# Fill and drain of a 41-beat pipeline: QKV products ahead of attention, spikes on GpSimd, filler products, four expert banks at the end

## The reference

```python
R, K, V = x @ Wr.T, x @ Wk.T, x @ Wv.T
r, k, v = lif(R), lif(K), lif(V)      # v = v + (x - v)/2 ; s = v >= 1 ; v = v*(1 - s), in time
h = 0.9*h + k*v ; y = r*h             # in time
x1 = LN1(x + y @ Wo.T)
s1 = lif(x1 @ W1.T + b1)              # width 1024
s2 = lif(s1 @ W2.T + b2)
x3 = LN(x + LN2(x1 + s2))             # LN3 in the kernel
g  = softmax(x3 @ Wg + bg) ; keep the top 2 of 8, renormalise
out = LN(x3 + sum_e g_e * (x3 @ We_e + be_e))    # all 8 experts are computed
```

## Time and profile before

| | us |
|---|---|
| median of 3 runs (lowest, highest) | 984.44 (983.77, 984.57) |
| the profiled execution's own time | 983.85 |
| its span, first to last instruction | 982.0 |
| granted TensorE clock, mean | 0.982 |

### The profile page before, as it was taken

How to read it: one execution, slowest core, us unless ns; L and a number is a source line. 1 busy time by engine, 2 the same in 40 slices (tenths; PEclk the granted TensorE clock), 3 DMA queues, 4 the chain that set the end, 5 groups by cost and what they waited for, 6 DMA issues and landing times.

```text
span 982.0 us, 20629 instructions
## 1 busy us (share of the span) xinstructions
PE 930.3 (95%) x6520; PEld 860.4 (88%) x6520; DVE 916.3 (93%) x3683; ACT 610.6 (62%) x1388; POOL 572.8 (58%) x730
## 2 busy tenths in 40 slices
PE   6878899999999999999999999999999999999985
PEld 5778789999999999999999999999999999788764
DVE  7699999999999999999999999999999999989865
ACT  6556455676666666766666667666666676555451
POOL 2222225666667766666677666667776666664552
PEclk9789999999999999999999999999999999999998
DMA  9543223455555544565555545655555455446763
GB/s 285 127 97 66 55 54 65 97 119 119 119 125 108 112 106 99 121 118 119 123 107 105 114 100 121 120 118 122 105 112 107 100 124 108 100 95 112 142 123 86
DMA packets 59293, 109.45 MB, mean 111 GB/s; under 512 B 6576, under 2 KB 6576, under 8 KB 59184
## 3 DMA queue, kind: packets, MB, share of 16 engines
q0 software_dynamic: 37584, 68.44, 40.8%
q1 hardware_dynamic: 16992, 31.30, 9.6%
q10 hardware_dynamic: 4608, 8.39, 2.3%
HBM read 31.29 MB, written 8.39 MB: 40 GB/s over the span
## 4 chain that ended last, share of the span: by engine, by line
PE 76%; DVE 14%; ACT 3%; issue 3%; DMA 2%; POOL 2%; SPq 0%; POOLq 0%; ACTq 0%; DVEq 0%
PE ps_e L405 29%; PE ps_proj L405 12%; PE ps_proj L480 10%; PE ps_proj L495 10%; PE ps_proj L501 5%; PE ps_attn L405 3%; DVE U L898 3%; DVE V L905 2%; PE ps_zx L459 2%; DVE stats L977 2%; PE ps_attn L459 1%; PE ps_attn L442 1%; DVE h L947 1%; DMA acc<-term 1%; POOL rstd L1337 1%
## 5 line engine op out<-in xcount | busy, mean ns | idle before, releaser
L405 PE MATMUL ps_e<-we_hi,x_hi 128*128 128x512 f32 (+2 forms) x640 | 229.6, 359 | 6.4 <-DVE acc L1120 2.8
L898 DVE SCALAR_TENSOR_TENSOR U<-V,U 128x256 f32<-128x256 f32 (+4 forms) x576 | 229.0, 398 | 3.9 <-ACT U L669 2.3
L905 DVE SCALAR_TENSOR_TENSOR V<-U 128x256 f32<-128x256 f32 (+4 forms) x576 | 225.5, 392 | 1.6
L405 PE MATMUL ps_e<-we_lo,x_hi 128*128 128x512 f32 (+2 forms) x640 | 224.0, 350 | 0.0
L405 PE MATMUL ps_e<-we_hi,x_lo 128*128 128x512 f32 (+2 forms) x640 | 223.2, 349 | 0.0
L1335 POOL TENSOR_SCALAR veps<-mv 128x2 f32<-128x2 f32 x128 | 49.7, 388 | 275.5 <-DVE mv L983 273.6
L1349 POOL TENSOR_SCALAR s<-U 128x256 fp32r<-128x256 f32 x208 | 192.8, 983 | 16.5 <-DVE V L905 16.5
L708 ACT ACTIVATE term<-ps_e,gate 128x256 f32<-128x256 f32 x372 | 160.3, 475 | 52.0 <-PE ps_e L405 50.9
L669 ACT ACTIVATE U<-ps_proj,cst 128x256 f32<-128x256 f32 x320 | 135.5, 480 | 70.5 <-PE ps_proj L501 62.0
L405 PEld LDWEIGHTS ps_e<-we_hi,x_hi 128*128 128x128 f32 x640 | 120.6, 188 | 22.6 <-DVE x_lo L1027 3.7
L654 ACT ACTIVATE U<-ps_proj 128x512 f32<-128x512 f32 x96 | 57.6, 600 | 129.7 <-PE ps_proj L405 129.7
(11 more groups left out here) (111 smaller groups left out, 2313.5 us busy)
## 6 DMA issues: line engine op xcount, KB each, us to landing
acc<-term POOLq DMA_DIRECT2D x93, 256.0 KB, 3.7
odd_sum<-term POOLq DMA_DIRECT2D x93, 256.0 KB, 3.3
xt<-x_T SPq DMA_DIRECT2D x33, 256.0 KB, 3.0
xa<-x_tok SPq DMA_DIRECT2D x32, 256.0 KB, 3.3
xb<-cst SPq DMA_DIRECT2D x32, 256.0 KB, 2.3
xb<-x_tok POOLq DMA_DIRECT2D x32, 256.0 KB, 6.1
xt<-x_hi POOLq DMA_DIRECT2D x31, 256.0 KB, 4.6
out<-res ACTq DMA_DIRECT2D x31, 256.0 KB, 2.0
```

Of the source, the lines that this page charges most:

```text
L405: mm = pe.matmul(dst, lhs, rhs, start=(i == 0), stop=(i == n - 1))
L898: v.scalar_tensor_tensor(out=U[:, s, t, c0:c1], in0=V[:, c0:c1], scalar=0.5, in1=U[:, s, t, c0:c1], op0=ALU.mult, op1=ALU.add).then_inc(do ...
L905: v.scalar_tensor_tensor(out=V[:, c0:c1], in0=u, scalar=THRESHOLD, in1=u, op0=ALU.is_lt, op1=ALU.mult).then_inc(done, 1)
```

## The change

It leaves beats 7 to 32 as they are and alters both ends.

* Beat 1: TensorE runs 46 filler matmuls into an unused bank ahead of attention, 4 ahead of x1_T, 8 after it and 8 more in `w1` ahead of the wait for `x1_lo`. VectorE has a table of its own, `FIRST_Y`, with the LN1 sum in slot 6, and `x1_low` in slot 23. ScalarE normalises and reads x1 earlier; the copy of Wo moves to the end of its beat, ahead of `low_x`.
* Beats 2 to 6: `rkv` part 0 (beat 2) or parts 0 and 1 (beats 3 to 6) come first in TensorE's beat, ahead of z_T and attention. From beat 3 on, `x1_T` comes after `w2`, and on ScalarE `read_x1` comes after `to_lif` of w2. `low_x` moves up, ahead of the third w1 part. GpSimd makes six of the eight spike tiles, at the head of its beat; VectorE makes two, in slot 2. LN1's sum, statistics and shift are in slots 4 to 10, `x1_low` in 19 (beat 6: 15).
* Drain: VectorE's `fin_stage` 0 to 3 move up in beats 33 and 34, and GpSimd adds term 7 ahead of LN3's deviation. Beats 35 to 37 (`tail`) have new lists on all engines: expert fills use four banks (two of `ps_e`, two of `ps_proj`), `expert0` comes after the experts and after z_T, terms 4 and 5 are added a beat earlier, and the scan of beat 35 runs in one piece between `fin_stage` 3 and the low half of x3. In beat 37 ScalarE and a DMA take fills 0 and 1, VectorE adds the others.

```diff
+BRIDGE_ATTN, BRIDGE_T, BRIDGE_W1 = 46, 4, 8
...
-FILL = dict(z_sum=-1, y=(-1,) * 5, spikes_h1=-1, fin_sum=-1,
+FILL = dict(z_sum=-1, y=(-1,) * 5, spikes_h1=2, fin_sum=-1,
             gate=(4, 5, 6, 7, 8, 10, 10, 11, 11, 12, 24, 26), add_e0=(13, 14),
-            ln1_sum=1, ln1_stats=(2, 3), ln1_aggr=4, ln1_norm=7, x1_low=17,
+            ln1_sum=4, ln1_stats=(5, 6), ln1_aggr=7, ln1_norm=10, x1_low=19,
             ln2_stats=(0, 0), ln2_aggr=1, ln2_scale=(5, 6), ln2_add=9,
...
             fin_add=24, fin_stats=25, fin_aggr=26, fin_shift=31)
-X1_LOW = {3: 19, 4: 19, 6: 15}
-DRAIN = dict(z_sum=-1, y=(-1,) * 5, spikes_h1=-1, fin_sum=11,
+FIRST_Y = dict(FILL, ln1_sum=6, ln1_stats=(7, 8), ln1_aggr=9, ln1_norm=13)
+X1_LOW = {1: 23, 6: 15}
+DRAIN = dict(z_sum=-1, y=(-1,) * 5, spikes_h1=-1, fin_sum=9,
              gate=(-1, -1, -1, -1, 0, 1, 2, 3, 4, 4, 6, 7), add_e0=(11, 12),
              ln1_sum=-1, ln1_stats=(-1, -1), ln1_aggr=-1, ln1_norm=4, x1_low=-1,
...
              ln3_stats=9, ln3_aggr=10, ln3_shift=14, x3_low=23,
-             fin_add=25, fin_stats=26, fin_aggr=27, fin_shift=31)
-TAIL = dict(DRAIN, add_e0=(5, 5), ln2_scale=(3, 4), x3_low=17)
+             fin_add=17, fin_stats=18, fin_aggr=19, fin_shift=31)
...
     def dve_spikes(self):
-        return FK if self.edge else 0
+        return FK if self.late else 2 if self.early else 0
...
+        def expert_bank(b, fill):
+
+            if not b.tail:
+                return ps_e[:, (b.slot(LAG_M, 2) * (E - 1) + fill) % 2]
+            i = ((E - 1) * (b.k - FIRST_TAIL) + fill) % 4
+            first = (FIRST_TAIL - LAG_M) * (E - 1) % 2
+            return ps_e[:, (first + i) % 2] if i < 2 else ps_proj[:, i - 2]
...
+                        if b.k == LAG_Y and f == 0 and e == 0:
+                            bridge(ps_e[:, 0, 0, :], BRIDGE_W1)
                         for k in range(DK):
                             if f == 0 and e == 0:
                                 pe.wait_ge(x1_lo_ready, b.value(DK, LAG_Y, k + 1))
...
             def expert(b, fill):
-                if some(b.value(E - 1, LAG_M, fill - 1)):
+                if b.tail and (b.k > FIRST_TAIL or fill > 1):
+                    if b.k == FIRST_TAIL and fill < 4:
+                        pe.wait_ge(proj_read, b.fills())
+                    elif b.last_m and fill == E - 2:
+                        pe.wait_ge(last_added, fill - 4 - 1)
+                    else:
+                        pe.wait_ge(term_ready, b.value(E - 1, LAG_M, fill - 3))
+                elif some(b.value(E - 1, LAG_M, fill - 1)):
                     pe.wait_ge(term_ready, b.value(E - 1, LAG_M, fill - 1))
-                bank = (b.slot(LAG_M, 2) * (E - 1) + fill) % 2
+                bank = expert_bank(b, fill)
...
+            def tail(b):
+
+                for part in (0, 1, 2, 3):
+                    expert(b, part)
+                if b.last_m:
+                    gates_T(b)
+                    for part in (4, 5):
+                        expert(b, part)
+                    biases(b)
+                    expert(b, 6)
+                    return
+                expert(b, 4)
+                gates_T(b)
+                x3_T(b)
+                for part in (5, 6):
+                    expert(b, part)
+                biases(b)
+                after = Beat(b.k + 1)
+                if after.has(LAG_Z):
+                    z_T(after)
+                expert0(after)
...
+                if b.tail:
+                    if b.has(LAG_M):
+                        tail(b)
+                    return
+                sooner = {LAG_Y + 1: 1}.get(b.k, 2) if b.early and b.k > LAG_Y else 0
+                for f in range(sooner):
+                    rkv(b, f)
                 if b.has(LAG_Z) and edge and b.k < FIRST_STEADY:
                     z_T(b)
...
-                    for f in range(3):
+                    for f in range(sooner, 3):
                         if f == 2 or edge:
                             rkv(b, f)
                     if b.k == LAG_RKV:
-                        bridge()
+                        bridge(ps_attn[:, 0, :], BRIDGE)
                     fill += 3
-                if b.has(LAG_Y) and b.early:
+                if b.k == LAG_Y:
+                    bridge(ps_e[:, 0, 0, :], BRIDGE_T)
+                if b.has(LAG_Y) and b.early and not b.has(LAG_S):
                     x1_T(b)
+                if b.k == LAG_Y:
+                    bridge(ps_e[:, 0, 0, :], BRIDGE_W1)
...
                     w2(b, fill)
                     fill += 1
+                if b.has(LAG_S) and b.early:
+                    x1_T(b)
                 if b.has(LAG_M) and not b.early and not b.ahead:
...
                 if b.has(LAG_M):
                     gates_T(b)
                     for part in (4, 5, 6):
-                        if part == 6 and b.last_m:
-                            biases(b)
-                        if part == 6 and b.late and not b.last_m:
-                            expert0(Beat(b.k + 1))
                         expert(b, part)
                         if part == 4 and b.has(LAG_Z) and b.late:
                             x3_T(b)
-                    if not b.last_m:
-                        biases(b)
+                    after = Beat(b.k + 1)
+                    if b.late and not after.tail:
+                        expert0(after)
+                    biases(b)
+                    if b.late and after.tail:
+                        z_T(after)
+                        expert0(after)
...
+            def tail(b):
+
+                if b.has(LAG_M):
+                    weigh(b)
+                    for part in (0, 1):
+                        read_expert(b, part)
+                if b.has(LAG_Z):
+                    for part in (2, 3):
+                        read_expert(b, part)
+                    norm_x3(b)
+                if b.has(LAG_M):
+                    turned_gates(b)
+                if b.has(LAG_Z):
+                    read_x3(b)
+                    for part in (4, 5, 6):
+                        read_expert(b, part)
+                leave(b)
+
+                if b.tail:
+                    tail(b)
...
                     for f in range(3):
                         to_lif(b, f, 2 * f * B, 2, None)
+                        if b.has(LAG_Y) and b.early and f == (0 if b.k == LAG_Y else 2):
+                            norm_x1(b)
                         if b.k == LAG_RKV and f < 2:
...
                     fill += 3
-                if b.has(LAG_Y) and b.early:
-                    norm_x1(b)
                 if b.has(LAG_M):
...
+                    weigh(b)
+                if b.k == LAG_Y:
+                    read_x1(b)
                 if b.has(LAG_X) and b.k > LAG_X:
                     split_x(b)
-                if b.k == LAG_Y:
-                    act.wait_ge(wo_loaded, 16)
-                    copy(wo_hi[:], wo[:]).then_inc(wo_hi_ready, 1)
                 if b.has(LAG_Y) and not b.early:
                     norm_x1(b)
-                if b.has(LAG_Y) and b.early:
+                if b.k == LAG_Y + 1:
                     read_x1(b)
                 for p in lowered_in(b.k):
                     weight_low(p)
...
                     to_lif(b, fill, COL_H2, 2, C_B2, -1.0)
                     fill += 1
+                if b.has(LAG_S) and b.early:
+                    read_x1(b)
                 if b.has(LAG_Z) and b.early:
                     norm_x3(b)
...
                         to_lif(b, fill + f, COL_H1 + 2 * f * B, 2, C_B1 + 2 * f)
                         for p in pieces_in(b.k)[f:f + 1]:
                             weight_high(p)
+                    if b.early and b.k > LAG_Y and b.has(LAG_X):
+                        low_x(b)
                 if b.has(LAG_Z) and b.early:
                     read_x3(b)
...
+            def next_sum(b):
+
+                dve.wait_ge(lif, b.value(2 * STEPS, 0, 2 * STEPS))
+                z_sum(Beat(b.k + 1), 0)
+                z_sum(Beat(b.k + 1), 1)
...
+                dve.wait_ge(zT_done, b.value(1, LAG_Z, 1))
+                bn_stats(1, 0, ps_zx[:, 0, :], ln2_steps)
+                bn_stats(1, 1, ps_zx[:, 1, :], ln2_steps)
+                bn_aggr(b, 1, ln2_steps, LN2_STEPS, LAG_Z, 2)
+                for step in range(4):
+                    gate_stage(b, step)
+                fin_stage(b, 0)
+                after(ln2_steps, LN2_STEPS, LAG_Z, b, 4)
+                ln2_scale(b, 0)
+                ln2_scale(b, 1)
+                for step in range(4, 10):
+                    gate_stage(b, step)
+                ln2_finish(b)
+                add_e0(b, 0)
+                add_e0(b, 1)
+                gate_stage(b, 10)
+                gate_stage(b, 11)
+                mean_shift(b, 2, ln3_steps, LAG_Z)
+                fin_stage(b, 1)
+                fin_stage(b, 2)
+                fin_stage(b, 3)
+                lif_to(STEPS)
+                x3_low(b)
+                if Beat(b.k + 1).has(LAG_Z):
```

(65 more changed lines are left out.)

151 lines of the change are left out of this document (97 added, 54 removed).

## The result

The kernel after takes 1000.09 us (median of 4 runs, 998.68 to 1001.61), the kernel before beside it 984.11 (983.45 to 984.57): ratio 1.0163, 95% interval 1.0142 to 1.0184. It is 16.0 slower; the forecast was 9 slower. The profiled execution took 998.68 with a span of 996.9, 14.9 longer than that of before.

A forecast was written before the change was run, and what follows sets the result against it. TensorE bounds the steady beats; the fill was costed from x1_lo to x1_lo. 983.85 + 8.0 (fill) + 1.2 (drain) = 993.0, so a median of 993.6 us; own range 987 to 998, for 8 in 10 runs 974 to 999.

The forecast's parts named there:

- beats 1 to 3: Fill: x1_lo ends near 35.0 in beat 1, at 54.5 to 56.3 in beat 2, 76.0 to 78.5 in beat 3.
- The signs named: Trace marks that would show the forecast right, among them VectorE standing 3 us or more for z_T in beat 6.
- the fill's +8.0: First 161 us: the new orders make the fill 4.4 to 11.5 us longer, taken as 8.0.
- the price of the low clock: TensorE: a pause of 2 us or more takes about 1.6 us from the following work, carried as an option.
- Beat 6: Fill: from x1_lo of beat 5 to that of beat 6 takes 31.4 to 33.0 us, against 25.0 before.
- Rival (B): Fill and drain: clock dips in four of six beats and late adds, 998 to 1003 us; chance 0.09.
- Rival (A): Fill: beat 1's 5.5 us gain survives if z_T of beat 6 is ready in time; near 976 us; chance 0.33.
- next to no idle time but the 3.0 us: VectorE in early beats before: almost never idle except 3.0 us ahead of beat 1's low half of x1.
- Spikes: VectorE, six tiles moved to GpSimd: gain 0.3 us per beat while the scan runs, 1.28 in beat 6.
- Drain: Last 121 us: beats 33 and 34 -0.6, 35 +2.7, 36 +1.7, last beat -2.6; sum +1.2, from -4 to +4.
- The bound of the one piece in beat 35: VectorE, drain: 32 dependent scan instructions at 0.22 us take 7.3 us; the beat takes 19.7, +2.7.

The follow-up runs named there:

- e12: e8 plus filler matmuls in TensorE's pauses of beats 2, 5 and 6 and `low_x` one step earlier in beat 1: 974.73 us, ratio to before 0.9916.
- e4: The kernel after plus filler matmuls in TensorE's pauses ahead of `w1` in beats 2 to 6: 993.64 us, ratio to before 1.0100.
- e2: The kernel after with beats 2 to 6 in the order of before and eight spike tiles on VectorE; new beat 1 and drain kept: 979.31 us, ratio to before 0.9946.
- e13: e2 with RKV put back ahead of z_T and attention, and `low_x` early, in beats 2 to 6: 989.22 us, ratio to before 1.0052.
- e14: e2 with only the later LN1 slots put back in beats 2 to 6: 984.32 us, ratio to before 1.0007.
- e15: e2 with only the late transpose and late read of x1 put back in beats 3 to 6: 987.19 us, ratio to before 1.0038.
- e7: e2 with six of eight spike tiles put back on GpSimd in beats 3 to 6: 980.42 us, ratio to before 0.9973.
- e3: The kernel before with the new drain alone, its fill unchanged: 984.06 us, ratio to before 1.0001.
- e8: e2 with beat 35's scan laid between VectorE's other instructions instead of in one piece: 972.88 us, ratio to before 0.9902.
- e6: The kernel after with z_T and attention ahead of all RKV in beat 6: 997.92 us, ratio to before 1.0154.
- e9: The kernel after with beat 6's z_T and attention ahead of all RKV, and x1 transposed ahead of `w2` and read first: 996.53 us, ratio to before 1.0138.
- e10: The kernel after with x1 transposed ahead of `w2` and read ahead of the weight copies in beats 3 to 6: 995.87 us, ratio to before 1.0125.
- e11: The kernel after with `low_x` of beat 1 read earlier, behind the second w1 part: 998.19 us, ratio to before 1.0154.
- e1: The kernel after with beat 6 alone in the order of before on every engine: 992.07 us, ratio to before 1.0077.
- e5: The kernel after with beat 6's x1 transposed ahead of `w2` and read ahead of the weight copies and expert reads: 997.63 us, ratio to before 1.0155.

## Why the prediction was wrong in size

* **The sign and the place were right.** A loss in the fill, most of it in beat 6, next to none in the drain. x1_lo ended where forecast in beats 1 to 3 (35.1, 55.4, 77.7 against 35.0, 54.5 to 56.3, 76.0 to 78.5). The signs named were seen (attention 1.97 in beat 1, 2.26 idle ahead of RKV in beat 2, 3.55 at LN2's statistics, x1 read behind the gates, 38.5 from the last z_T to the end), but for one: the first steady beat began 14.7 later, not 5 to 11.
* **The step that failed is the fill's +8.0.** It was +14.7, and the term mis-sized in it is the price of the low clock. It shows in three places. (1) x1_lo of beat 5 came at 125.0, not about 122.4: +2.6. (2) Beat 6 took 34.2, not 31.4 to 33.0: +2.0. Its z_T began 15.2 behind x1_lo instead of 12.6 to 14.2, since `w1` of beat 5 took 8.2. From the end of z_T to x1_lo it was 18.4, close to the forecast's 18.1. (The terms listed for it add up to 17.8. One of them grew: GpSimd took 2.85 us for LN1's deviation, 147.49 to 150.34, and before 1.2.) (3) `w1` of beat 6: 8.15, not about 6.0: +2.2. Together 6.8.
* **What the low clock costs.** I carried "about 1.6 us from the work in it", from one short spell, and as an option of `w1` (5.2 to 6.8). But `w1` took 8.2 in beats 5 and 6, 2.4 above full clock, because the new order puts two or three pauses of TensorE right ahead of it. In the old order the pause lies ahead of `w2`, and there full clock gained nothing (e12): the same low clock, at no price. e4 measured it: 6.4 us. With the pauses filled x1_lo of beat 5 comes 87.7 behind that of beat 1 (after 89.8; the forecast 87.4), beat 6 takes 31.9, inside the forecast, and the time is 993.64. That this is the 993.6 of the forecast is in part luck: the fill was still 9.7 later than before, the drain nothing instead of +1.2.
* **What is left open.** In the profiled execution the fill was 6.7 over the forecast and the drain some 1.3 under it. Two of the four runs were 2.8 longer than that execution, and no profile shows where. Rival (B), 998 to 1003, had the time and half of the mechanism (low clock in `w1`), not its late adds in the drain, and got 0.09.
* **Rival (A)'s mechanism is true, its condition was not met.** The gain of beat 1 survives all five beats if their order stays (e2, -4.5); it was lost to the new orders, as the forecast said. What it did not see is that three parts of them each cost by themselves (e13 to e15), the LN1 slots too, which I took as fitting the later attention. (Its "next to no idle time but the 3.0 us" of VectorE before also leaves out 3.47 us ahead of LN1's sum of beat 1 and 2.26 at the start of scan 2; its sum does not hang on them.)
* **Spikes.** Forecast was a gain of 0.3 per beat; measured was a loss of 1.1 in four beats by medians, within what can be told from nothing, and no difference between the marks of the traces (e7). That the slowing eats the gain was right.
* **Drain.** +1.2 was forecast; e3 has +0.3 as the difference of medians, with an interval of -1.1 to +1.3, so the sum is not refuted. Its terms one by one: beats 33 and 34 gained 1.1 (forecast 0.6), beat 35 took 19.0 (19.7), and from the last z_T to the end it took 38.5, 0.9 less than before, as forecast. The bound of the one piece in beat 35 was right and showed the remedy.

## What to carry to other kernels

When an engine is busy 94% of a stretch (VectorE in 41 to 161 us before) and the chain from beat to beat runs over four engines, an order that starts one product earlier is paid by the instruction that now stands behind it. Price every swap by what VectorE, the bound, will wait for, and each pause of TensorE by the product that follows it: here one ahead of work whose end is waited for (`w1`) cost its low clock in full, one ahead of covered work (`w2`) nothing. Test a bundle of changes part by part before it goes in together; here beat 1's part gave 4.5 us, those of beats 2 to 6 cost 20.8, and the drain's made no difference until e8 mended it.

## What the hardware did that I had not expected

* After the same pause of 2.26 us, TensorE's clock fell in three executions and held in three (0.58 to 0.61 and 1.00 over the same 4 us), and five executions of the same fill code came to x1_lo of beat 5 between 125.0 and 128.4. The Trainium skill (TensorE: Matmul & The Clock Gate, Part 1: The HAM clock gate) says that the activity monitor runs freely and not from the kernel's start, so that the same code can meet it at another point; by that rule both results are to be expected, and the six profiles agree in that they show both; where the monitor stood no trace shows.
* GpSimd's two small LN1 instructions took 1.12 and 1.65 us in beat 6 of after, 0.38 and 0.71 in beat 6 of before. They did so again in e4, e6, e9, e10 and e11, which have after's VectorE table in that beat, and not in e1 and e13, which have the old one; in e5 only the first was long (1.18 and 0.80). The cause is not shown.
* Small dependent instructions of VectorE start 0.225 us apart; with one of another chain between each two, 0.11:

```profile
950.82 0.19 DVE L993 SCALAR_TENSOR_TENSOR U<-V,U 128x32 f32<-128x32 f32 x1
951.05 0.19 DVE L1000 SCALAR_TENSOR_TENSOR V<-U 128x32 f32<-128x32 f32 x1
951.27 0.19 DVE L993 SCALAR_TENSOR_TENSOR U<-V,U 128x32 f32<-128x32 f32 x1
```
```profile
923.18 0.19 DVE L1027 SCALAR_TENSOR_TENSOR V<-U 128x32 f32<-128x32 f32 x1
923.29 0.16 DVE L1188 RECIPROCAL gweight<-gden 128x2 f32<-128x2 f32 x1
923.41 0.19 DVE L1020 SCALAR_TENSOR_TENSOR U<-V,U 128x32 f32<-128x32 f32 x1
```

The first is the kernel after in beat 35, the second e8. That, and not the waits (VectorE idle 1.1 and 0.8 us), is where the 4 us of beat 35 came from: the piece that ran alone shrank from 7.1 us to 2.6, and the stretch ahead of it, with 20 scan instructions laid in, grew only from 9.7 to 10.2.
